# A fused graph-attention and transformer layer on one core: the order of steps in each engine's round

## What is computed

```python
self_feat = concat([x, q_exp]) @ W_self.T + b_self
for d in range(2):
    aff = where(cond > 0, qh @ kh / 4, NEG) + label_bias      # 16 heads, 20 keys
    output += (softmax(aff) @ kv) @ Wout[d] + bout[d]
x1 = x + relu(output)
```

```python
nx = ada_rmsnorm(x1, cond);  q, k, v = nx @ wq, nx @ wk, nx @ wv
x2 = x1 + softmax(rope(q) @ rope(k).T / 4) @ v @ wo
nz = ada_rmsnorm(x2, cond)
out = x2 + (gelu(nz @ w_gate) * (nz @ w_up)) @ w_down
```

## Time and profile before

| | us |
|---|---|
| median of 3 runs | 656.99 |
| lowest and highest | 651.46, 657.21 |
| profiled execution: span, first to last instruction | 653.9 |
| mean granted TensorE clock, share of full | 0.896 |

### The profile page before, as it was taken

The page is one execution under the profiler, slowest core; times in us unless marked ns, Lnnn a source line. Parts: engine busy times, 40 slices in busy tenths (PEclk is TensorE's granted clock), DMA queues, the critical chain, the costliest instruction groups (busy, mean ns, idle before and its releaser), DMA issues.

```text
span 653.9 us, 10746 instructions
## 1 busy us (share of the span) xinstructions
PE 533.7 (82%) x3780; PEld 449.7 (69%) x3780; DVE 401.3 (61%) x752; ACT 222.7 (34%) x421; POOL 223.6 (34%) x185
## 2 busy tenths in 40 slices
PE   2868837889798979897989799879989697768667
PEld 0757725669686878686868786778778685666457
DVE  5576837467666776775867576767666653544112
ACT  2232110544144324523263416340634153203320
POOL 1161460146321643155215620462245321421012
...
DMA packets 36169, 40.00 MB, mean 61 GB/s; under 512 B 3328, under 2 KB 32552, under 8 KB 35888
## 3 DMA queue, kind: packets, MB, share of 16 engines
...
...
## 4 chain that ended last, share of the span: by engine, by line
PE 45%; DVE 19%; DMA 14%; issue 8%; SPq 5%; POOL 4%; ACT 4%; DVEq 0%; POOLq 0%; ACTq 0%
PE ps L1167 16%; DMA kst<-qk_d 9%; PE ps L1413 7%; PE ps L1429 5%; PE ps L1388 5%; DVE nm L1010 5%; DMA qk_d<-ya 4%; SPq L328 3%; PE ps L1329 3%; PE ps L1317 2%; PE ps L1302 2%; POOL splz L411 2%; SPq L325 1%; DVE xr L961 1%; DVE msk L841 1%
## 5 line engine op out<-in xcount | busy, mean ns | idle before, releaser
L1010 DVE TENSOR_REDUCE nm<-ps 128x2 f32<-128x512 f32 x128 | 83.2, 688 | 42.4 <-PE ps L1388 42.2
L1167 PE MATMUL ps<-splz,wh 128*128 128x256 f32 x512 | 101.9, 297 | 7.7 <-POOL splz L411 6.4
L1388 PE MATMUL ps<-kst,qst 96*128 96x256 f32 x256 | 62.5, 354 | 42.9 <-DMA kst<-qk_d 37.7
L1167 PEld LDWEIGHTS ps<-splz,wh 128*128 128x128 f32 x512 | 84.4, 202 | 9.7 <-issue 7.0
L411 POOL TENSOR_TENSOR hs<-g,hs 128x512 fp32r<-128x512 f32 x32 | 41.0, 1280 | 125.1 <-DVE hs L742 125.1
L638 ACT ACTIVATE ya<-ps 128x512 f32<-128x512 f32 x128 | 69.5, 595 | 40.4 <-PE ps L1413 38.9
L1388 PEld LDWEIGHTS ps<-kst,qst 96*128 96x128 f32 x256 | 46.1, 231 | 53.4 <-DMA kst<-qk_d 21.8
L1167 PE MATMUL ps<-splz,wl 128*128 128x256 f32 x256 | 75.0, 293 | 0.0
L675 ACT ACTIVATE g<-ps 128x512 f32<-128x512 f32 x32 | 19.1, 598 | 140.9 <-PE ps L1167 140.8
L1413 PE MATMUL ps<-qst,kst 100*128 100x256 f32 x256 | 54.6, 324 | 4.8 <-issue 1.7
L1167 PE MATMUL ps<-wh,hs 128*128 128x256 f32 x256 | 57.2, 300 | 1.0 <-POOL hs L411 1.0
...
## 6 DMA issues: line engine op xcount, KB each, us to landing
...
```

The lines of the kernel that those rows point to most:

```text
L1010: dve.tensor_reduce(nm[:, :, h], ps[:, h % 2].rearrange("p (c s) -> p c s", c=TC), AX.X, ALU.max, negate=True).then_inc(mx_ok.sem, 1)
L1167: ins = pe.matmul(dst, lhs(a, k), rhs(c, k), start=first_ and n == 0 and m == 0, stop=last_ and n == len(ks) - 1 and m == 2, **kw)
L1388: ins = pe.matmul(ps[:, bk, c * S:(c + 1) * S], qst[0:96, h // 2, c * P:(c + 1) * P], kst[0:96, h, :], start=True, stop=True)
```

## The change

On all five engines the list in `round_` is put into another order. No step is added, taken away or changed within; the waits stay in the steps. Some steps pass the border of a round: on POOL asub(1) is now at the end of the round before, x1bias at the top of the next; on ACT aexp(1) and nrowc are at the top of the next; on PE pTt(0) is at the end of the round before. Some once-only steps pass it too. Batches stay in order, since each such step's batch shifts along (`it` becomes `it + 1` or `it - 1`). The diff, indentation taken out:

```diff
@@ -349,42 +349,42 @@
...
-  once(weights("qk", 1), it)
+  once(weights("qk", 1), it + 1)
+  once(get_bo, it + 1)
+  once(get_wsm, it)
   once(weights("q0", 0), it + 1)
-  once(weights("g", 2), it)
+  once(weights("g", 1), it)
   once(weights("u", 2), it)
+  once(get_consts, it + 1)
+  once(get_wc2, it)
+  once(get_rope, it)
+  once(weights("u", 3), it)
+  once(weights("d", 3), it - 1)
+  once(weights("u", 0), it)
+  once(get_brow, it + 1)
+  once(cond, it + 1)
+  once(weights("v", 0), it + 1)
   once(get_wb, it + 1)
-  once(get_brow, it + 1)
-  once(weights("u", 0), it)
-  once(weights("u", 3), it)
+  once(weights("self", 0), it + 1)
   step(load_adj, it + 1)
-  once(cond, it + 1)
-  once(weights("self", 0), it + 1)
-  once(weights("d", 2), it - 1)
-  once(get_wc2, it)
-  once(get_consts, it + 1)
+  step(load_x, it + 1)
   once(weights("g", 3), it)
-  step(load_x, it + 1)
-  once(weights("u", 1), it)
-  once(weights("d", 0), it)
-  once(get_rope, it)
+  once(weights("qk", 0), it + 1)
+  once(weights("u", 1), it + 1)
+  once(qrows, it + 1)
+  once(weights("o", 0), it + 1)
   step(load_x_add, it)
   once(weights("q0", 1), it + 1)
-  once(weights("v", 0), it + 1)
+  step(load_q, it + 1)
+  once(get_angles, it + 1)
+  once(weights("d", 0), it)
+  once(weights("g", 0), it + 1)
+  step(stack, it)
   once(weights("d", 1), it)
-  once(weights("qk", 0), it + 1)
+  once(weights("d", 2), it)
+  step(nrows, it)
   once(get_vec, it + 1)
-  once(weights("d", 3), it - 1)
-  once(weights("o", 0), it + 1)
-  once(qrows, it + 1)
-  once(get_angles, it + 1)
-  once(get_bo, it + 1)
-  step(load_q, it + 1)
-  step(stack, it)
-  once(weights("g", 1), it + 1)
-  step(nrows, it)
-  once(weights("g", 0), it + 1)
-  once(get_wsm, it + 1)
+  once(weights("g", 2), it + 1)
   step(store, it - 1)
...
@@ -495,37 +495,37 @@
...
-  step(asub(1), it)
-  once(fills, it + 1)
   step(aprob(1), it)
-  once(wlow("g", 1), it)
+  step(x1bias, it - 1)
+  step(pow1, it)
   once(wlow("d", 2), it - 1)
   once(wlow("g", 2), it)
-  step(pow1, it)
+  once(fills, it + 1)
+  step(alow, it - 1)
   once(wlow("o", 0), it + 1)
-  once(wlow("d", 0), it)
-  once(wlow("d", 3), it - 1)
-  step(alow, it - 1)
   step(nxl, it)
   step(selfl, it + 1)
-  step(pow2, it - 1)
+  once(wlow("d", 3), it - 1)
   step(radd(0), it)
   step(radd(1), it)
-  once(wlow("d", 1), it)
+  once(wlow("d", 0), it)
+  step(pow2, it - 1)
   step(qklow(0), it)
-  once(wlow("g", 0), it + 1)
   step(nzl, it - 1)
   step(qklow(1), it)
+  step(hlow(0), it - 1)
   step(aadd(0), it + 1)
-  once(wlow("g", 3), it)
-  step(hlow(0), it - 1)
+  step(hlow(1), it - 1)
   step(asub(0), it + 1)
   step(aadd(1), it + 1)
+  step(hlow(2), it - 1)
+  once(wlow("g", 0), it + 1)
+  once(wlow("g", 3), it)
+  once(wlow("g", 1), it + 1)
   step(aprob(0), it + 1)
-  step(x1bias, it)
-  step(hlow(1), it - 1)
-  step(hlow(2), it - 1)
+  once(wlow("d", 1), it)
   step(hlow(3), it - 1)
+  step(asub(1), it + 1)
...
@@ -676,62 +676,62 @@
...
+  once(whigh("g", 1), it)
+  step(nrowc, it - 1)
+  once(whigh("qk", 1), it + 1)
+  step(aexp(1), it)
   step(exph(0), it - 1)
   step(exph(1), it - 1)
-  once(whigh("u", 2), it)
-  once(whigh("qk", 0), it + 1)
-  once(whigh("self", 0), it + 1)
+  once(whigh("v", 0), it + 1)
+  once(whigh("u", 0), it)
+  once(whigh("u", 3), it)
   step(exph(2), it - 1)
   step(exph(3), it - 1)
-  once(hidden_cond, it)
   step(exph(4), it - 1)
   step(exph(5), it - 1)
+  once(hidden_cond, it)
   step(exph(6), it - 1)
   step(exph(7), it - 1)
-  once(whigh("g", 2), it)
   step(exph(8), it - 1)
   step(exph(9), it - 1)
   step(exph(10), it - 1)
   step(exph(11), it - 1)
-  once(whigh("d", 2), it - 1)
   step(oc(0), it - 1)
+  once(whigh("g", 2), it)
   step(exph(12), it - 1)
-  once(whigh("d", 0), it)
   step(exph(13), it - 1)
-  once(whigh("g", 3), it)
+  once(whigh("self", 0), it + 1)
   step(exph(14), it - 1)
   once(whigh("q0", 0), it + 1)
-  once(whigh("u", 3), it)
   step(exph(15), it - 1)
-  once(whigh("o", 0), it + 1)
   step(oc(1), it - 1)
   step(square1, it)
-  once(whigh("d", 3), it - 1)
   step(xh, it + 1)
   step(nzt, it + 1)
+  once(whigh("g", 3), it)
+  once(whigh("u", 1), it + 1)
   once(whigh("q0", 1), it + 1)
-  once(whigh("d", 1), it)
+  once(whigh("o", 0), it + 1)
+  once(whigh("d", 3), it - 1)
   step(nxc, it)
+  once(whigh("d", 0), it)
   step(selfc, it + 1)
   step(square2, it - 1)
-  step(vcopy, it)
-  once(whigh("qk", 1), it + 1)
-  step(kvrep, it + 1)
-  once(whigh("v", 0), it + 1)
-  once(whigh("g", 0), it + 1)
   step(q0c(0), it + 1)
   step(nzc, it - 1)
   step(q0c(1), it + 1)
   step(gelu(0), it - 1)
   step(gelu(1), it - 1)
-  once(whigh("g", 1), it + 1)
+  step(gelu(2), it - 1)
+  once(whigh("u", 2), it + 1)
+  once(whigh("qk", 0), it + 1)
   step(aexp(0), it + 1)
-  step(gelu(2), it - 1)
+  once(whigh("d", 1), it)
+  once(whigh("g", 0), it + 1)
+  step(kvrep, it + 1)
+  step(vcopy, it)
   step(gelu(3), it - 1)
-  once(whigh("u", 0), it + 1)
-  once(whigh("u", 1), it + 1)
-  step(nrowc, it)
-  step(aexp(1), it + 1)
+  once(whigh("d", 2), it)
...
@@ -1079,57 +1079,54 @@
...
+  once(wlow("u", 2), it)
+  once(wlow("u", 1), it)
+  once(qrow_parts, it + 1)
+  once(wlow("u", 0), it)
   step(asums(1), it)
   step(pTc(0), it)
   step(pTc(1), it)
-  once(wlow("u", 2), it)
+  step(pTc(3), it)
   step(pTc(2), it)
-  step(pTc(3), it)
+  once(wlow("v", 0), it + 1)
   step(adjm, it + 1)
-  once(qrow_parts, it + 1)
+  once(table, it)
+  step(yadd, it)
+  step(x1add, it)
+  once(wlow("self", 0), it + 1)
+  step(nz, it + 1)
+  once(zeros(1), it + 1)
+  step(cur_1, it)
+  step(v1_in, it)
+  once(wlow("q0", 0), it + 1)
+  step(onorm(0), it - 1)
+  step(onorm(1), it - 1)
   once(wlow("u", 3), it)
-  step(yadd, it)
-  step(nz, it + 1)
-  once(wlow("q0", 0), it + 1)
-  step(x1add, it)
-  once(zeros(1), it)
-  step(onorm(0), it - 1)
-  step(v1_in, it)
-  step(onorm(1), it - 1)
   step(xl, it + 1)
-  once(wlow("self", 0), it + 1)
   step(xr_scaled, it)
   step(aadd32, it - 1)
-  once(table, it)
+  step(cur_2, it - 1)
+  step(nxh, it)
   once(wlow("q0", 1), it + 1)
-  step(cur_1, it)
-  once(zeros(0), it + 1)
-  step(nxh, it)
-  once(rotated_bias, it)
+  step(mask, it + 1)
+  once(rotated_bias, it + 1)
+  step(selfh, it + 1)
   step(x2add, it - 1)
-  step(selfh, it + 1)
-  step(v2_in, it - 1)
   step(rot(0), it)
   step(rot(1), it)
-  step(mask, it + 1)
+  step(v2_in, it - 1)
   step(xr2_scaled, it - 1)
-  once(wlow("qk", 0), it + 1)
+  once(ones(0), it + 1)
   step(qkadd(0), it)
   step(nzh, it - 1)
-  once(ones(1), it)
-  once(ones(0), it + 1)
   step(qkadd(1), it)
-  step(cur_2, it)
-  once(wlow("qk", 1), it + 1)
   step(kb, it + 1)
-  once(wlow("v", 0), it + 1)
-  once(bout, it + 1)
   step(am(0), it + 1)
   step(hmul(0), it - 1)
+  step(hmul(1), it - 1)
+  step(am(1), it + 1)
+  once(ones(1), it)
   step(amax(0), it + 1)
-  step(am(1), it + 1)
-  step(hmul(1), it - 1)
-  step(asums(0), it + 1)
   step(mx(0), it)
   step(mx(1), it)
   step(mx(2), it)
@@ -1138,22 +1135,25 @@
   step(mx(5), it)
   step(mx(6), it)
   step(mx(7), it)
-  step(hmul(2), it - 1)
+  step(asums(0), it + 1)
   step(mx(8), it)
+  once(wlow("qk", 1), it + 1)
   step(mx(9), it)
-  once(wlow("u", 0), it + 1)
   step(mx(10), it)
   step(mx(11), it)
+  step(hmul(2), it - 1)
+  once(wlow("qk", 0), it + 1)
+  once(bout, it + 1)
   step(mx(12), it)
   step(mx(13), it)
   step(mx(14), it)
   step(mx(15), it)
   step(nmx, it)
+  step(hmul(3), it - 1)
   step(amax(1), it + 1)
-  step(hmul(3), it - 1)
+  once(zeros(0), it + 1)
   step(vb, it + 1)
   step(result, it - 1)
-  once(wlow("u", 1), it + 1)
...
@@ -1502,102 +1502,102 @@
...
+  step(pTt(1), it)
   step(st(1), it - 1)
-  step(pTt(0), it)
   step(st(2), it - 1)
   step(st(3), it - 1)
-  step(pTt(1), it)
   step(st(4), it - 1)
-  once(cond_1, it)
   step(st(5), it - 1)
   step(pv(0), it - 1)
   step(st(6), it - 1)
+  step(pTt(3), it)
   step(st(7), it - 1)
   step(pTt(2), it)
-  step(pTt(3), it)
   step(st(8), it - 1)
   step(st(9), it - 1)
-  once(cond_q, it + 1)
+  once(cond_2, it)
   step(pv(1), it - 1)
   step(st(10), it - 1)
   step(st(11), it - 1)
   step(y, it)
   step(st(12), it - 1)
-  once(cond_2, it)
   step(st(13), it - 1)
   step(pv(2), it - 1)
   step(st(14), it - 1)
   step(st(15), it - 1)
+  once(cond_q, it + 1)
   step(x1T, it)
   step(pv(3), it - 1)
   step(xT, it + 1)
   step(oT(0), it - 1)
   step(oT(1), it - 1)
   step(nzTt, it + 1)
+  step(adjT, it + 1)
   step(aT, it - 1)
   step(selfm(0), it + 1)
   step(nxT, it)
   step(selfm(1), it + 1)
+  step(wo(1), it - 1)
   step(wo(0), it - 1)
-  step(wo(1), it - 1)
-  step(adjT, it + 1)
   step(qk(0), it)
   step(qk(1), it)
   step(v(0), it)
+  step(q0(0, 1), it + 1)
   step(q0(0, 0), it + 1)
-  step(q0(0, 1), it + 1)
-  step(v(1), it)
   step(qkT(0), it)
+  step(q0(1, 0), it + 1)
   step(nzTr, it - 1)
+  step(k0, it + 1)
   step(qkT(1), it)
-  step(q0(1, 0), it + 1)
-  step(k0, it + 1)
   step(q0(1, 1), it + 1)
```

(35 more changed lines are left out.)

## The result

The changed kernel takes 682.9 us (median of 4 runs, 681.5 to 684.6) beside 657.1 for the kernel before (4 runs, 651.5 to 658.2): slower by 3.9% by the medians. The ratio on record with its 95% interval is 1.054 [1.044, 1.064]; it lies above every ratio of the times listed here (684.6 / 651.5 = 1.051 at most), and the record does not show how it was formed, so the size is known to some 4 to 5%, the sign without doubt. The forecast was 680. The profiled execution grew from 653.9 to 681.7 us, by 27.8.

The account below looks back on a forecast made before the run. TensorE (82% busy) is not the sole bound: a 68.3 us round chain counts six or seven times. Terms sum to +22.8 on the 653.9 us span, 676.7, plus 3.1: 680; forecast 671 to 689 (chance 0.47), wider range 663 to 693.

Parts of the forecast that it names:

- the 3.1 us that the forecast added to the span: Excess of the shown median over the 653.9 us profiled span, added to the forecast span 676.7 to give 680.
- splz: Sign of a right forecast: its low half on POOL, once a round, comes every 69.5 to 70.3 us.
- The s/mx loop: From s(0) to nmT: asums between mx(7) and mx(8) and reordered TensorE products cost +0.75 us a round, bounds 0 and 1.1.
- the walk through the heads: Step through the loop's 16 heads at 0.645 us per mx, putting nmT at 15.35 us after s(0) instead of 14.6.
- From nmT to st(0): Leg after the loop: the DMAs end it at 4.95 us, so taking TensorE work away gains 0.
- The st stage: st/exp/pv stage: down(3,1) and pTt(1) before st(1) delay exp(1) and pv(0); +1.1 us a round, 0.3 to 1.4.
- pv(3) to the stack: Last pv to q/k store: moved adjT and mask gain, xr2_scaled and qkT(1) wait; -0.2 us a round, bounds -1.3 and +0.3.
- The once-only low half d3: First round with batches 0 and 2: wlow d3 behind selfl delays square2 and the radds, +1.3 us once.
- The start: Before the first steady round: moved once-only steps and load waits cost +10.8 us, bounds 4 and 18.
- The tail's 0.7: End of the kernel: the last hlow now covers two downs instead of three, +0.7 us.
- Only the start is worse: Rival: stalls absorb asums and the exps catch up, rounds stay at 68.3 us; total 669, chance 0.17.
- Faster: Rival: mask and adjT before qkadd(0) give 1.3 us a round, the loop absorbs the rest; total 650, chance 0.07.

Follow-up runs that it names:

- e4: Changed kernel with the old order in rounds -1 and 0 of every engine, the new order in rounds 1 to 8: 669.2 us, ratio 1.025.
- e5: New order in rounds -1 and 0 of every engine, the old order in rounds 1 to 8: 668.8 us, ratio 1.028.
- e7: Changed kernel with 36 matmuls, result unread, added before s(0) in each of batches 1 to 7: 669.6 us, ratio 1.029.
- e12: e7 with asums(0) moved back ahead of mx(0): 665.9 us, ratio 1.018.
- e10: Kernel before with 20 matmuls, result unread, added before s(0) in each of batches 1 to 7: 650.9 us, ratio 0.986.
- e6: Kernel before with only TensorE's order from s(0) to nmT as in the changed kernel: 667.4 us, ratio 1.028.
- e2: Changed kernel with up(2,0), down(0,0) and up(2,1) back in their old TensorE places in the s/mx loop: 675.1 us, ratio 1.030.
- e1: Changed kernel with asums(0) alone moved back ahead of mx(0): 676.5 us, ratio 1.036.
- e3: Changed kernel with TensorE's order around st(0) as before (down(3,1), pTt(0), pTt(1), pTt(3) back): 683.6 us, ratio 1.042.
- e8: Kernel before with mask, adjT, v2_in, pow2 moved, xr2_scaled behind qkadd(0), and nzh, nzl, nzTr behind the q and k steps: 655.2 us, ratio 1.005.
- e11: e10 with asums(0) alone moved between mx(7) and mx(8), run once: 695.9 us.
- e9: e8 with xr2_scaled back ahead of qkadd(0): 648.2 us, ratio 0.982.

## Why the prediction was right, and where it was off

**Direction and size.** Right, by 2.9 us in the medians; by 5.0 in the profiled execution, where 22.8 was forecast and 27.8 measured, since the 3.1 us that the forecast added to the span were only 1.2 (682.9 less 681.7). Part of that closeness is luck: the loop cost 8.4 us more than forecast, the leg from nmT to st(0) 0.6 and that before the stack 0.5 more, and the reload, the st stage and the tail took 3.0, 0.9 and 0.6 less. Of the three large terms only the st stage came out by its own steps. e4 and e5 show that start and rounds contribute independently, as the sum took them to. Of the signs that were named, asum between two mx, pv(0) 3.5 us after the first exp, qkadd(0) behind xr and x1add at 74.94 came; `splz` stood 68.0 to 72.2 us apart instead of 69.5 to 70.3, and nmT came 15.2 to 15.5 us after s(0) in one middle round of six.

**The s/mx loop (forecast +0.75 a round, measured +1.9 in the middle ones).** This is the term that was mis-sized. Its mechanism is there, and at equal clock its size too: 0.70 for asums (e7 less e12), some 0.2 for the order (e12 against e10), and 15.37 against 14.6 us in the two loops whose low stretch ended at 3.4 and 3.5 us. A low stretch that ends 3.4 to 4.5 us behind s(0) adds 1.3 us to the full-clock loop in either order (14.5 less 13.2, 15.4 less 14.1); one that ends at 7.7 to 9.8 us adds 2.0 to 3.2 to the new one. What failed is the walk through the heads, which used the clock of the kernel before as given, although showed 0.89 over the loop. In the new loop VectorE waits 0.84, 0.29, 1.01 and 0.84 us for a TensorE at half speed. e6 shows that the order of the products alone brings it, e2 that moving three of them back takes part of it away, e7 that without it the excess is gone. Why the clock comes back earlier in one order than in the other was not settled; TensorE is busy for 8.60 of the first 8.96 us of the loop shown, so it is not idleness that one sees in these rows. Nor does the clock tell all of the time from run to run: of the changed kernel's four runs two had a mean granted clock of 0.93 and 0.92 over the span and took as long (spans 680.5 and 682.8) as the two at 0.89 (681.7 and 679.7). By an estimate from these shares and spans, the first two had some 95 and 105 us at 1.2 GHz, the profiled one 157, and nothing of the difference is in the time. What took it there is open; one execution of each kernel has a trace. What rests on medians is e2 (-8), e7 (-13), both across chips, and e6 (+12 on the kernel before, same chip).

The overlap seen in e1 was missed as well: the longer TensorE is slow, the less asums costs.

**From nmT to st(0) (forecast 0).** Right: 4.88 to 5.05 us in the middle rounds (before 4.93 to 4.96), fewer products or not, and the DMA still ends it. The table's 0.6 is for the most part the last round (5.83 against 5.36), where TensorE waits 1.93 us for the last hlow.

**The st stage (+1.1 a round, measured +0.89).** Right in kind: ScalarE idles behind the first exp, pv(0) comes 0.77 later, the rest 0.12; e3 takes exactly this back in the stage, though not in the time. The spacing of the second part was put at 0.2 and is half that.

**pv(3) to the stack (-0.2, measured -0.07 in the middle rounds).** Right in size: v1_in costs 0.14 before alow, and qk(0) comes 0.2 earlier after it. From qk(0) to qkadd(0) it stays at 6.95 us (6.93 before): xr2_scaled, which waits 1.95 us for pow2, takes back all that the moved mask could give. qkT(1) holds qkadd(1) by 0.37, but from qkadd(0) to the store it stays at 4.50. That v2_in would end with the second radd did not come: it took 0.17 us at 229.30, and the radds ran from 228.15 to 230.74.

**The once-only low half d3 (+1.3, measured +0.1).** This term was wrong. In the first round with batches 0 and 2 the low half ran from 156.62 to 157.91 and radd began at 157.88; from alow to the store it took 14.72 us, in the next rounds 14.62. The 1.4 us that the same leg grew by, 16.79 against 15.40, are in the last full round: between the last pv and the store TensorE had 6.8 us at 1.2 GHz there, before 3.4. The table's line hides these two misses.

**The start (+10.8, measured +10.8).** The exact agreement is luck. The first alow came at 134.2 to 140.6 us in the seven traces with the old start (before, e4, e6, e8 to e11) and at 145.7 to 151.5 in the seven with the new (after, e1 to e3, e5, e7, e12), some of them with a small edit of their own in that part; on average they are 11.0 apart, so the size of the sum holds, but a single pair could have shown 5 or 17. Within the two executions read here two misses cancel. x1add of batch 0 came at 74.94, not at 72.5. A part was there from the first steps: adjm began at 13.12, where my sum had it at about 12.0, after a wait for its own load, and self began at 21.88, 5.8 later than before and not 4.9. The rest came later:

```profile
13.12 0.89 DVE L820 TENSOR_TENSOR aff<-adjC,wb 80x704 f32<-80x704 int32 x1 [1.93 <-DMA adjC<-adj]
...
48.00 1.35 DVE L789 TENSOR_TENSOR wl<-xr,wh 128x512 fp32r<-128x512 f32 x1
49.27 1.78 DVE L789 TENSOR_TENSOR wl<-x,wh 128x512 fp32r<-128x512 f32 x1
50.97 1.22 DVE L773 TENSOR_TENSOR vec<-vec 128x2 f32<-128x2 f32 x1
52.12 0.81 DVE L893 TENSOR_REDUCE amx<-aff 128x32 f32<-128x640 f32 x1
53.30 1.76 DVE L746 MEMSET kst<- 96x2048 f32 x1 [0.38 <-issue]
54.99 0.62 DVE L919 TENSOR_TENSOR vblk<-ps,const_sb 128x512 f32<-128x512 f32 x1
...
74.94 0.69 DVE L940 TENSOR_TENSOR x<-ps,x_add 128x512 f32<-128x512 f32 x1 [1.27 <-PE ps L1207]
```

```profile
47.52 2.98 POOL L406 TENSOR_TENSOR wl<-ya,wh 128x512 fp32r<-128x512 f32 x2
50.47 1.71 POOL L443 TENSOR_TENSOR prob<-aff,arc 128x640 f32<-128x640 f32 x1
```

amax(1) and vblk stand behind low halves that I priced at 0.7 us and behind a memset (zeros(0), 1.76) that I left out. The low halves take 1.35 and 1.78 us beside POOL's, and an operation on 128 x 2 elements takes 1.22 us and ends, at 52.19, with POOL's aprob, at 52.18. The Trainium skill ("SBUF — State Buffer", Who interferes with whom) has VectorE and GpSimd lock a shared port pair against each other; the trace agrees, and I had used it for one row of the steady round and not for the start. The other miss went the other way: the first st stage ran at 2.4 GHz throughout, where 6.8 us of it had been at 1.2 before, and from st(0) to alow it took 20.0 us instead of 22.7. This second miss belongs to these two executions: from st(0) to the last pv the fourteen traces take 14.4 to 17.5 us, 15.4 on average with the old start and 15.2 with the new.

```profile
117.90:140.62 22.72, 20.53 (x162) 14.62 (x162) 13.73 (x28) 12.33 (x26) 4.54 (x5) 0.85 0.21 66
```

```profile
131.37:151.39 20.02, 18.56 (x166) 12.45 (x166) 13.05 (x29) 12.26 (x25) 4.47 (x4) 1.00 0.21 61
```

**The rest.** The tail's 0.7 did not appear (0.1). The reload took 3.0 us less in seven rounds, most of it in the last two; it varied between 12.8 and 14.9 us from store to s(0) before and between 12.7 and 14.5 after, and no run was aimed at that.

**The rivals.** "Only the start is worse" fell with e4 and e5. "Faster" counted on the mask, and in the changed kernel xr2_scaled takes its gain back; e8, with xr2_scaled behind qkadd(0), shows 0.4 us a round of it, and e9 got its earlier stack without it. That a longer low-clock stretch would double the loop's cost was no rival of mine, and should have been one.
